# Low output halves and the norm's iteration on GpSimd, feed-forward term in PSUM, values product in 32-column weights, second queries in the first stage

## The reference

```
xn = layernorm(x)
q = xn @ Wq (16 heads of 64); latent = xn @ Wkv_down (64)
k = latent @ Wk_up; v = latent @ Wv_up
attn = softmax(causal(q k^T / 8))
x = x + (attn v) @ Wout + tanh(xn @ weight @ aux1 @ aux2 + bias)
```

## Time and profile before

| what | value |
|---|---|
| runs of before, us | 2001.54, 2001.67, 2013.03 (median 2001.67) |
| profiled execution, us | 2006.04 |
| its span, first to last instruction, us | 2004.3 |
| mean granted clock of TensorE in it | 0.99 of full speed |
| TensorE (matmul) busy | 1966.3 us, 98% |
| GpSimd busy | 1482.9 us, 74% |
| VectorE busy | 1360.3 us, 68% |
| ScalarE busy | 1157.7 us, 58% |

### The profile page before, as it was taken

How to read it: one execution, slowest core, us unless ns; L and a number is a source line. 1 busy time by engine, 2 the same in 40 slices (tenths; PEclk the granted TensorE clock), 3 DMA queues, 4 the chain that set the end, 5 groups by cost and what they waited for, 6 DMA issues and landing times.

```text
span 2004.3 us, 34226 instructions
## 1 busy us (share of the span) xinstructions
PE 1966.3 (98%) x11208; PEld 1327.7 (66%) x11208; DVE 1360.3 (68%) x3619; ACT 1157.7 (58%) x2203; POOL 1482.9 (74%) x1291
## 2 busy tenths in 40 slices
PE   8999999999999999998999999999999999999997
PEld 6766666676666676765666666666767666676754
DVE  5778665796667765687666876668756687565761
ACT  4565565565555565564565555655656556565653
POOL 0677677786777777875777877778768787777786
PEclk8999999999999999999999999999999999999998
DMA  4222122221222212221121221222221222121210
...
DMA packets 117825, 116.48 MB, mean 58 GB/s; under 512 B 24208, under 2 KB 100880, under 8 KB 117648
## 3 DMA queue, kind: packets, MB, share of 16 engines
...
## 4 chain that ended last, share of the span: by engine, by line
PE 91%; DVE 5%; ACT 2%; issue 1%; DMA 0%; POOL 0%; ACTq 0%; DVEq 0%; POOLq 0%; SPq 0%
PE ps L996 25%; PE ps L932 21%; PE ps L1010 14%; PE ps L980 13%; PE ps L983 12%; PE ps L1034 3%; DVE split_lo L1253 1%; DVE ps L1232 1%; PE ps L1023 1%; ACT probs L1140 1%; PE ps L1063 1%; ACT q_hi L1202 0%; DVE maxima L1237 0%; DVE acc L1281 0%; PE ps L809 0%
## 5 line engine op out<-in xcount | busy, mean ns | idle before, releaser
L1377 POOL TENSOR_TENSOR p_sum<-p_sum,probs 128x512 f32<-128x512 f32 x672 | 868.7, 1321 | 129.9 <-ACT probs L1140 127.7
L1140 ACT ACTIVATE probs<-ps 128x512 f32<-128x512 f32 x1152 | 667.7, 597 | 335.5 <-PE ps L983 320.6
L1232 DVE CUSTOM_DVE_ANT_0 ps<-ps,causal 128x512 f32<-128x512 f32 (+4 forms) x1024 | 521.0, 527 | 196.7 <-PE ps L1010 188.3
L996 PE MATMUL ps<-probs,latent 128*64 128x512 f32 x2304 | 518.1, 597 | 0.0
L980 PE MATMUL ps<-q_hi,k_hilo 128*128 128x512 f32 x1152 | 474.8, 412 | 6.9 <-ACT probs L1140 3.2
L1010 PE MATMUL ps<-k_hilo,q_hi 128*128 128x512 f32 (+4 forms) x1536 | 473.9, 356 | 2.8 <-DVE maxima L1232 1.2
L983 PE MATMUL ps<-q_lo,k_ones 65*128 65x512 f32 x1152 | 457.8, 397 | 0.0
L1377 POOL TENSOR_TENSOR p_sum<-probs 128x512 f32<-128x512 f32 x224 | 294.3, 1328 | 202.9 <-ACT probs L1140 202.2
L1237 DVE TENSOR_REDUCE maxima<-ps 128x1 f32<-128x512 f32 (+1 forms) x512 | 326.1, 637 | 147.3 <-PE ps L1010 143.6
L996 PEld LDWEIGHTS ps<-probs,latent 128*64 128x64 f32 x2304 | 156.2, 137 | 301.0 <-issue 297.6
L1010 PEld LDWEIGHTS ps<-k_hilo,q_hi 128*128 128x128 f32 x1536 | 282.6, 190 | 97.3 <-DVE maxima L1232 18.2
...
## 6 DMA issues: line engine op xcount, KB each, us to landing
q_hi<-q_hi SPq DMA_DIRECT2D x256, 128.0 KB, 2.4
norm<-recips SPq DMA_DIRECT2D x256, 128.0 KB, 2.9
q_lo<-q_lo SPq DMA_DIRECT2D x128, 128.0 KB, 2.3
...
q_lo<-rows SPq DMA_DIRECT2D x128, 4.0 KB
rows<-norm SPq DMA_DIRECT2D x128, 4.0 KB
```

Source lines behind the costliest of these rows:

```text
L996: last = nc.tensor.matmul(y_bank[g * LATENT:(g + 1) * LATENT, :], latent[par][:, key_block(unit, s), :], probs[:, t % PT_SLOTS, g * BANK:( ...
L1140: nc.scalar.activation(probs[:, t % PT_SLOTS, g * BANK:(g + 1) * BANK], ps[:, bank_of[kind, key], :], ACT.Exp).then_inc(exp_done, 1)
L1232: nc.vector.tensor_tensor_reduce(bank, bank, causal[:, BANK - w:BANK], 1.0, LOWEST, ALU.add, ALU.max, maxima[:, unit % 4, h, 0:1]).then_in ...
L1377: nc.gpsimd.tensor_tensor(sums, other, probs[:, slot, part], ALU.add).then_inc(pool_done, 1)
```

## The change

- `WIDTHS["PV"]` 64 becomes 32: a PV is four matmuls with 32-column weights instead of two with 64. The work is the same.
- `LO` moves from DVE to POOL. In `LN1`, four steps stay on DVE; the Newton rounds go to POOL and, since each round is four instructions there and not three, are 12 and not 9. `LN4` goes to POOL. DVE no longer waits for each step of the norm inside its own queue: the semaphore `ln_chain` is awaited ahead of the next one.
- `F` stays in its PSUM bank: bias added in place, tanh in place, and `FA` adds from PSUM. The bank is free after `FA`, not after the bias. `F` no longer waits for the `FA` before it.
- The queries (1,0) and (1,1) are made in `first_plan` instead of the body, in banks 4 and 3; `MT` 0 goes to bank 2; "fold wff" comes behind the last maxima.
- Planner: `LEAD` 13 becomes 10; late work is taken ahead of an `ST` unless it is late by no more than 2.5 steps and ACT has been idle for 300 ns (before: late by no more than 0.5 steps and ACT free within 300 ns); cost tables follow the moves.

```diff
-LN1_PARTS = 13
+LN1_PARTS = 16
-WIDTHS = {"PV": 64, "R": 32}
+WIDTHS = {"PV": 32, "R": 32}
-LEAD = 13
+LEAD = 10
...
-            if half == 0 and b == 0:
-                out += [(0.3, "Q", (1, 0)), (1.6, "Q", (1, 1))]
...
             elif kind == "LN1":
-                end = self.run("DVE", when, DVE_TIME[kind])
+                end = self.run("POOL", when, (350, 450)) if key[1] >= 4 else self.run("DVE", when, (300, 400))
...
             elif kind == "LN4":
-                self.xn[key] = self.run("DVE", when, DVE_TIME[kind])
+                self.xn[key] = self.run("POOL", when, (1400, 1500))
...
             elif kind == "LO":
-                self.normal[key] = self.run("DVE", when, DVE_TIME[kind])
+                self.normal[key] = self.run("POOL", when, (1300, 1350))
...
-            if self.n_f < len(self.f) and (self.n_f < 1 or self.f[self.n_f - 1][1] in self.added):
+            if self.n_f < len(self.f):
...
-            idle_act = self.free["ACT"] < now + 300
+            idle_act = self.free["ACT"] < now - 300
             late = max(due, key=lambda c: step - c[1], default=None)
-            if late and (not st or step - late[1] > 0.5 or not idle_act):
+            if late and (not st or step - late[1] > 2.5 or not idle_act):
...
-    plan += [("W", "fold wvo"), *maxima[3:6], ("W", "fold wff"), *maxima[6:]]
-    plan += [("MT", 0), ("W", "split wvo")]
+    plan += [("W", "fold wvo"), *maxima[3:6], *two_parts("Q", (1, 0)), *maxima[6:]]
+    plan += [("W", "fold wff"), ("MT", 0), *two_parts("Q", (1, 1)), ("QL", (1, 0)), ("QD", (1, 0))]
+    plan += [("W", "split wvo"), ("QL", (1, 1)), ("QD", (1, 1))]
...
                 elif kind == "F":
-                    wait_new(f_biased, count.of(kind, key) + 1)
+                    wait_new(ff_added, count.of("FA", key) + 1)
...
-                        last = nc.tensor.matmul(y_bank[g * LATENT:(g + 1) * LATENT, :],
-                                                latent[par][:, key_block(unit, s), :],
-                                                probs[:, t % PT_SLOTS, g * BANK:(g + 1) * BANK],
-                                                start=(s == 0), stop=(s == block_of(unit)))
+                        for half in range(0, LATENT, WIDTH):
+                            row = g * LATENT + half
+                            last = nc.tensor.matmul(y_bank[row:row + WIDTH, :],
+                                                    latent[par][:, key_block(unit, s), half:half + WIDTH],
+                                                    probs[:, t % PT_SLOTS, g * BANK:(g + 1) * BANK],
+                                                    start=(s == 0), stop=(s == block_of(unit)))
...
-                    nc.scalar.activation(ff[:, :], ff[:, :],
-                                         ACT.Tanh).then_inc(tanh_done, 1)
+                    f_bank = ps[:, bank_of["F", key], 0:D]
+                    nc.scalar.activation(f_bank, f_bank, ACT.Tanh).then_inc(tanh_done, 1)
...
+                elif kind == "LO":
+                    slot = key % SPLIT_SLOTS
+                    pool.wait_ge(norm_hi, key + 1)
+                    nc.gpsimd.tensor_tensor(split_lo[:, slot, :], y[:, key % Y_SLOTS, :],
+                                            split_hi[:, slot, :].bitcast(F32),
+                                            ALU.subtract).then_inc(norm_lo, 1)
+                elif kind == "LN1" and key[1] >= LN1_BITS:
...
+                    pool.wait_ge(ln_chain, chain_at(b, n))
+                    part = (n - LN1_BITS) % 4
+                    if part == 0:
+                        done = nc.gpsimd.tensor_tensor(square, last, last, ALU.mult)
+                    elif part == 1:
+                        done = nc.gpsimd.tensor_tensor(scale, square, var, ALU.mult)
+                    elif part == 2:
+                        done = nc.gpsimd.tensor_scalar(scale, scale, -0.5, 1.5, ALU.mult, ALU.add)
+                    else:
+                        done = nc.gpsimd.tensor_tensor(guess, scale, last, ALU.mult)
+                    done.then_inc(ln_chain, 1)
```

87 lines of the change are left out of this document (37 added, 50 removed).

## The result

The changed kernel takes 2013.43 us (median of 20 runs, 2010.66 to 2014.93), the kernel before 2001.61 us beside it (20 runs, 1993.25 to 2037.0): a ratio of 1.0057, 95% interval 1.0044 to 1.0069, 11.8 us slower. The forecast was 1997, 5 us faster than before: the measured time lies within the stated range (1974 to 2024) but above the forecast's own 1987 to 2012, and on the other side of before. The profiled execution took 2012.04 us with a span of 2010.1.

The account below looks back on a forecast made before the run. The prediction took TensorE, busy 98% of the span, as the bound. Its seven terms summed to -9.4 us, taking the profiled 2006.04 us to 1996.6; it forecast 1997, range 1974 to 2024.

Parts of the forecast that it names:

- term 4: Norm's iteration and block scaling on GpSimd: first stage's path gets longer, +2.2 us (bounds 0.5 and 5).
- rival B: GpSimd becomes the bound, its in-order queue holding masks and sums that TensorE needs: 2032 us, chance 0.18.
- term 5: split_lo off VectorE: two TensorE waits and the clock's fall behind the long one go, -9.1 us.
- term 1: TensorE's turns between array widths: 0.14 us saved a trip, half given back by 21 more trips, -6.6 us.
- term 2: Values product as four 32-column matmuls side by side: nearly the same speed, +1 us (bounds -2 and +10).
- Term 3: Second queries made in the first stage, in TensorE's gaps, instead of the body: -2.6 us, or 0 if not hidden.
- Term 6: Small TensorE waits under the new planner order, more on exp, fewer on maxima: +3 us (bounds -15 and +12).
- Term 7: Tail waits for split_lo and last row sums grow; feed-forward bank held longer counted 0: +2.7 us (bounds 0, +6).
- A: Rival: VectorE's freedom shrinks TensorE's small waits everywhere, giving 1979 us; chance 0.22.
- C: Rival: array turns cost the same at any width change, so 21 more trips lose 7 us: 2010, within the forecast's 0.6.

Follow-up runs that it names:

- e1_first_norm_dve: The changed kernel with batch 0's norm (Newton rounds and scaled blocks) back on VectorE, every order kept: 2002.08 us.
- e2_fill_gap: The changed kernel with seven matmuls on constants, results unread, filling TensorE's wait for GpSimd in the first stage: 2006.68 us.
- e4_pv32_only: The kernel before with only the values product made 32 columns wide, in the order of before: 1987.62 us.
- e6_q_first_only: The kernel before with only the second queries moved to the first stage, the order behind planned anew by the old rules: 2011.86 us.
- e8_pv32_q_first: The kernel before with 32-column values products and the second queries moved to the first stage: 1999.68 us.
- e9_all_norms_dve: The changed kernel with the norms of all eight batches on VectorE, every order kept: 2021.22 us.
- e16_blocks_dve: The changed kernel with batch 0's norm and all other batches' scaled blocks on VectorE, their iteration left on GpSimd: 2010.01 us.
- e5_lo_pool_only: The kernel before with only split_lo moved from VectorE to GpSimd, all orders kept: 2128.79 us.
- e3_lo_dve: The changed kernel with only split_lo put back on VectorE, all orders kept: 2075.82 us.

## Why the prediction was wrong

**Two steps failed, and either alone eats the predicted gain of 5 us.** One is term 4, +2.2 in the sum and +11.3 measured. Had it come at 2.2, the kernel would stand near 2004, still behind before. The other is the wait for the mask, rival B's mechanism, some 10 us, for which the sum had no term (below).

**Term 4 failed.** "With one tensor read instead of two I take 0.4 each" is the step: GpSimd needs 1.21 us for a scaled block, three times the 0.4 taken and 1.7 times the upper bound of 0.7. The row for it was drawn from a selection of 64 columns and a product of 512, by columns alone. One tensor less does not make it faster: 256 columns with two scalars per partition take nearly as long as 512 of a product of two tensors (1.28). Whether the scalars are what costs, no run separates. The Trainium skill (GPSIMD Engine Reference, "Elementwise — side-by-side cycle accounting") gives about 2.6 cycles an element for an operation on two tensors, from which, at the 1.2 GHz that the section reckons with, I estimate some 0.55 us for 256. The rows show 1.21 for one tensor and two scalars, and the measurement decides. The small steps were right: 0.28 for the 0.30 taken. The later start itself, 17.27 for 12.71, is 4.6 us, still within the term's bound of 5. The second half of the failure is that this wait was priced at its own length: the clock fell in it, and 27 us of the first stage ran at 0.60. The term measured +11.3 (e1_first_norm_dve), 6.7 of it the clock (e2_fill_gap), each within some 4 us. The prediction had counted just such a fall in term 5, for the earlier trace rows, and had not looked for it here.

**Terms 1 and 2 were right.** The narrow quads take 0.431 us, R follows at once, and a batch became 1.6 to 2.0 us shorter (1.7 by term 1). That the 13.6 us saved at the turns came as 14.1 in the medians (e4_pv32_only) is closer than the 6 us of their interval allow, and so in part luck. The 12 trips that the planner adds came as 2.7 us (4 by term 1), less than the runs can tell from nothing. The 21 trips of the changed kernel were never run alone. The extra 9 us that the prediction worked out from the Trainium skill (TensorE: Matmul & The Clock Gate, "Measured speedup vs the span model") did not come: with them e4_pv32_only would have been near 1997, outside its interval.

**Term 3 is open in size.** By the profiles the queries in the first stage cost nothing up to product 36 in e6_q_first_only and e8_pv32_q_first, and gave nothing either. The predicted 2.6 us is below what a new order does by itself. The second wait before the first score product did not go, it became 1.16 us. That product came 14.6 us later, not 2 to 3, about half of it by term 4 (7.7 in the profile of e1_first_norm_dve). Where neither term 4 nor the clock is in the way it comes at 51.8 and 52.7 (e9_all_norms_dve, e16_blocks_dve), 1.3 and 2.2 later than before, near what the prediction said.

**Term 5 was right in the trace, not as a gain.** No split_lo takes over 1.32 us now, the long stall and the fall of the clock at 930 us are gone. Its sign "no VectorE instruction of several us" did not hold: one step of the norm takes 3.9 us in six of the seven later batches (last section), and nothing waits for it. (The spread of the runs went from 44 us to 4; that the one comes of the other is not shown.) But the edit needs the order that belongs to it: on its own it costs 127 us (e5_lo_pool_only), undone in the new order 62 (e3_lo_dve), so it has no price of its own.

**Term 6 was off by size and by place.** Waits on exp went down (36.2 to 25.2 us of idle loader), not up. Instead the masks came (9.4 us), and the loader's two rows of waits for maxima together rose from 24.5 us (18.2 and 6.3) to 34.8 (16.8 and 18.0). Three and more products for maxima stand directly behind one another 105 times in the new order, 86 times in the old. Terms 1, 2, 5 and 6 were to give 11.7 us in the body; it gave the 2.8 of the first table. The mask in six batches, 10 us, is of the size of what is missing.

**Term 7** was +2.7 and is +0.7 by the table: the three waits for split_lo in the tail are 6.9 us, where they were 5.6 (13.2 less the two that term 5 names).

**The rivals.** A did not come: VectorE is idler by 213 us, and the loader waits for its maxima more, not less. B's mechanism is there, GpSimd at 84% (82 to 87 was forecast), busy without a gap for 25 us and more in each batch, PV behind a mask. Its price is 1.7 us in each of six batches, 10 in all, not 35. It was at 0.18, and the forecast had no term for it; together with term 4, which is the same misjudged instruction (eight blocks of 1.21 are 9.7 us of a batch), it is where a good part of the gain went. C, as the prediction has it (a trip costs the same by either way, so nothing is won), fell with e4_pv32_only, which would have stayed at 2001.

**The range.** With the bounds of terms 2, 4 and 6, as the prediction says, it ends at 2017.5; the 2024 needs the upper bounds of term 7 as well. The measured 2013.4 lies within either, though term 4 left its own bounds.

**What stays open.** That the mask's wait is caused by the scaled blocks is shown (without them it goes). That its removal would be worth 10 us is not, since each time the work was moved, VectorE took as much. How much of the body's missing gain is due to the planner's new order itself cannot be separated by undoing a part: each undone part brought another order, worth between +2.7 and +41 us, or was put into an order that did not fit it. An order in which only the masks stand ahead of the scaled blocks in GpSimd's queue was not run; it is the next thing to try.
